# Routing a mixture of experts in four parts, with token lists kept in DRAM

## Chip, cores and metric

The kernel runs on one core of a Trainium2 chip. The metric is the device time of one launch in microseconds. The engines are TensorE (PE, with its weight loads shown as PEld), VectorE (DVE), ScalarE (ACT), GpSimd (POOL) and SyncE (SP, which issues most DMAs). Each engine runs its own instructions in program order and waits on semaphores.

## What is computed

The input is 8 batches of 512 tokens of 256 channels. Each batch goes through a linear attention layer, and then all 4096 tokens go through a feed-forward layer with one shared expert and 8 routed ones, of which every token uses two.

```python
x = x + layernorm(attention(layernorm(x)))          # per batch: q, k, v; state = k'v; ctx = q state; group norm; out
xf = layernorm(x).reshape(-1, 256)
shared = ffn(xf, shared_gate, shared_up, shared_down)   # ffn = (silu(x g') * (x u')) d', 704 hidden channels
probs = softmax(xf @ gate_w.T)                          # 8 experts
topw, topi = top_k(probs, 2);  topw = topw / topw.sum()
comb[token, topi] += topw
routed = sum over experts e of ffn(xf, e) * comb[:, e]
x = x + layernorm(shared + routed)
```

## The kernel before

The program has three stages. In the first, batch by batch, attention is computed, and beside it the shared expert of the batch before. The second, the **tail**, holds the shared expert of the last batch and all of the routing that is left. The third, the **routed stage**, works on 39 tiles (`NTILE`) of 256 token rows (`TW`), each of one expert. Tiles 0 to 7 belong to experts 1 to 8 in turn, so their weights are known without the routing; for the rest a table `eid` says which expert.

The order of the first two stages is written out by hand: `ORDER` for batches 1 to 6, `LAST_ORDER` for batch 7 and `TAIL`. Every engine walks the same list and does its share of each step. `("G", c)` is a gate and up projection on PE (12 matmuls, L911), `("H", c)` what ACT and DVE do with it (silu at L723, product at L1218, a high half at L737 and a low half at L1228), `("D", c)` the down projection on PE (L926). A batch has twelve of each. PE may start a G only when the product of the G two before is made, since there are two PSUM banks.

Four steps of a batch need a reciprocal root, which POOL computes (`root`, L605), in this order: LN1 at `ln1_stats`, the group norm GN at `ctx_norm`, LNO at `lno_stats` and LN2 at `x2`. DVE waits for them at L1207, L1414, L1428 and L1438. PE's output projection (L1015) needs what DVE makes at L1418. After LN2, ACT normalises the rows, which are then turned, give the routing logits and feed the next batch's shared expert.

The routing logits are in `logits`, a tile of 128 tokens to 8 columns. `route` runs on DVE in two parts: part 0 is batches 0 to 6 (28 tiles, 224 columns), part 1 is batch 7 (4 tiles, 32 columns). `route_probs` subtracts the maximum (L1317, L1318), ACT takes the exponential (L775), `route_top1` normalises and finds the first expert, `route_top2` the second and the weights. Part 0 runs in batch 7, part 1 at the end of it and in the tail. Then, in the tail:

- `route_slots`: PE counts with two matmuls (L1040, L1041), and DVE makes from them the place of each token in its expert's list (L1459 to L1474).
- `route_order` and `route_table`: the experts of tiles 8 to 38.
- `route_positions`: for each token its two places, split in a high and a low part.
- `one_hots` and `invert`, eight times: for four tiles of tokens DVE and POOL write one-hot matrices of the low part (L1527, L642), DVE those of the high part (L1530, 624 columns), and PE sums their products (L1052). The result has the token number of each place of all 39 tiles.
- `route_indices`: DVE turns that into indices for gathers (`idx`, L1550) and for scatters (`idx_s`, L1549).

POOL then gathers the rows of a tile by an indirect DMA (`gather_x`, L661), SP turns them by DMA, and the routed stage starts. The result of each tile is added to `acc_d` in DRAM by an indirect DMA with an add (`scatter`, L672). The profile names the DRAM tensor `xn2_d` as `xn_d` and `x2_d` as `x_d`.

During the first tiles of the routed stage the weights of experts 7 and 8 are still being laid out (`LATE`).

Of the kernel before, what the change touches and what calls it, by code (L numbers as in the profile page):

```python
# [8 lines left out]
F32 = mybir.dt.float32  # L9
# [7 lines left out]
P = 128  # L17
# [44 lines left out]
def turned_before(b, by_pe):  # L62
# [7 lines left out]
LAST_ORDER = [("ctx",), ("G", 0), ("ctx_out",), ("G", 1), ("channel_stats",), ("H", 0), ("group_mean",), ("H", 1), ("G", 2), ("group_var",),  # L70
# [5 lines left out]

TAIL = [("route_top1", 1), ("route_top2", 1), ("G", 0), ("H", 0), ("route_slots",), ("G", 1), ("G", 2), ("H", 1), ("D", 0), ("G", 3),
         ("D", 1), ("route_order",), ("G", 4), ("G", 5), ("H", 2), ("G", 6), ("G", 7), ("route_positions",), ("H", 3), ("route_table",),
         ("H", 4), ("G", 8), ("D", 2), ("one_hots", 0), ("G", 9), ("H", 5), ("H", 6), ("invert", 0), ("one_hots", 1), ("H", 7),
         ("invert", 1), ("D", 3), ("D", 4), ("one_hots", 2), ("invert", 2), ("one_hots", 3), ("H", 8), ("invert", 3), ("one_hots", 4),  # L80
         ("invert", 4), ("one_hots", 5), ("D", 5), ("invert", 5), ("G", 10), ("one_hots", 6), ("D", 6), ("H", 9), ("D", 7), ("invert", 6),
         ("one_hots", 7), ("invert", 7), ("G", 11), ("route_indices",), ("H", 10), ("D", 8), ("H", 11), ("D", 9), ("D", 10), ("D", 11)]
# [28 lines left out]
PROGRAM += [(b, step) for b in range(1, B - 1) for step in ORDER if b < NPRE or not step[0].startswith("prep")]  # L111
# [5 lines left out]
def build(nc, x_in, gu_in, dn_in, wqkv_in, wout_in, cols_in, out):  # L117
    xf = x_in.rearrange("b s d -> (b s) d")
    of = out.rearrange("b s d -> (b s) d")
    with ExitStack() as ctx:  # L120
# [10 lines left out]
        acc_d = nc.dram_tensor("acc_d", (TOK + TT * P, D), F32, kind="Internal").ap()  # L131

# [85 lines left out]
        OHB, POOL_H = 4, 1  # L218
        OHG = NTB // OHB
        OHR = 4  # L220
        oh_lo = [(wdn[:, (E - 1) * SLOT_DN + n * 1024:(E - 1) * SLOT_DN + (n + 1) * 1024] if n < OHR - 1 else attw[:, 2048:2560].bitcast(F16)).rearrange(
            "p (m h c) -> p m h c", m=2, h=OHB) for n in range(OHR)]
        OHI = 2 * OHB * NCOL
        OHS = 5
        oh_hi = [(spare[:, 2 * KD * S + n * OHI:2 * KD * S + (n + 1) * OHI] if n < OHS else xhl[:, (n - OHS) * OHI:(n - OHS + 1) * OHI]).rearrange(
            "p (m h c) -> p m h c", m=2, h=OHB) for n in range(OHG)]
# [90 lines left out]
        counted = sem("counted")  # L317
        eid_made = sem("eid_made")
# [81 lines left out]
        READ |= {KV_USES[t]: (kv_made, NT, t + 1) for t in range(NT)}  # L400

# [31 lines left out]
        def _(sp):  # L433
# [84 lines left out]
            sp.wait_ge(comb_made, 2)  # L518
            sp.dma_start(xn2_d[:, D:D + E].rearrange("(t p) e -> p t e", p=P), r_t.rearrange("p (t e) -> p t e", e=E)).then_inc(comb_stored, 16)
# [51 lines left out]
        def _(pool):  # L571
# [7 lines left out]
            g.iota(iota_i, pattern=[[1, P]], base=0, channel_multiplier=0).then_inc(link_p, 1)  # L579
            pool.wait_ge(link_p, 7)  # L580
# [1147 lines left out]
```

## Time and profile before

| | us |
|---|---|
| median of 3 runs | 857.74 (857.69 to 858.41) |
| the profiled execution | 856.2, of which span 854.4 |
| PE busy | 776.4 |
| DVE busy | 586.5 |
| ACT busy | 485.1 |
| POOL busy | 290.0 |

The profile is of one execution; times in it count from the start of its span. A batch of the first stage takes 40.95 us; batch 5 is at 223.4 to 264.3, batch 7 from 305.3 to 346.2, the tail to 396, and the routed stage's first matmul is at 402.6. An idle time in square brackets is that of the engine just before the row, with what ended it.

### The profile page before, as it was taken

What the parts mean: (1) busy time and instruction counts of PE and PEld (TensorE: products, weight loads), DVE (VectorE), ACT (ScalarE), POOL (GpSimd) and SP (SyncE); (2) the same over time, 40 slices, a digit from 0 to 9 for tenths busy, and PEclk for the clock granted to TensorE, in tenths of its full rate; (3) what the DMA queues carried; (4) which work ended last, traced back from release to release, by engine and by line L of the source; (5) the groups of instructions that cost most, each with busy time, mean ns of one, the idle gap of its engine ahead of it and who ended that gap; (6) DMA issues with size and microseconds to landing.
All of it is one profiled execution on the core that took longest, in us unless ns stands there. A gap on an engine that the chain in (4) does not pass through costs nothing.

```text
span 854.4 us, 20946 instructions
## 1 busy us (share of the span) xinstructions
PE 776.4 (91%) x6525; PEld 641.2 (75%) x6526; DVE 586.5 (69%) x1591; ACT 485.1 (57%) x1068; POOL 290.0 (34%) x316
## 2 busy tenths in 40 slices
PE   3679999999999998675899999999999999999991
PEld 1447777777777776554787888888888888888880
DVE  6668889898989888894787544555555555555553
ACT  2264848485857575522566555565656565656562
POOL 3011010101010100062265555555555555555542
PEclk9899999999999999987999999999999999999996
DMA  4104444454435342502244644646464646474843
GB/s 191 50 25 180 105 148 113 142 124 154 131 136 150 105 149 81 148 1 69 50 71 71 102 73 74 122 77 148 71 147 73 147 66 147 73 145 71 149 41 97
DMA packets 102690, 90.08 MB, mean 105 GB/s; under 512 B 63760, under 2 KB 94224, under 8 KB 101456
## 3 DMA queue, kind: packets, MB, share of 16 engines
q1 hardware_dynamic: 87648, 68.45, 28.0%
q0 software_dynamic: 14976, 20.78, 16.5%
q8 instruction: 38, 0.62, 0.3%
q14 instruction: 28, 0.23, 0.1%
HBM read 48.70 MB, written 27.39 MB: 89 GB/s over the span
## 4 chain that ended last, share of the span: by engine, by line
PE 73%; DVE 15%; ACT 5%; issue 3%; DMA 2%; POOL 1%; SPq 0%; ACTq 0%; DVEq 0%; POOLq 0%
PE ps L911 41%; PE ps L926 19%; PE ps L983 4%; PE ps L1015 3%; DVE wgu L1278 3%; PE ps L977 2%; ACT wgu L771 2%; DVE hf L1218 1%; DVE wdn L1278 1%; DVE st L1394 1%; PE ps L952 1%; DVE st L1198 1%; DVE wdn L1527 1%; PE ps L986 1%; DVE hT L1228 1%
## 5 line engine op out<-in xcount | busy, mean ns | idle before, releaser
L911 PE MATMUL ps<-xhl,wgu 128*128 128x256 f16 x3102 | 386.1, 274 | 12.2 <-DMA xhl<-attw 6.6
L911 PEld LDWEIGHTS ps<-xhl,wgu 128*128 (+1 forms) x3102 | 303.3, 98 | 55.7 <-issue 8.8
L1218 DVE SCALAR_TENSOR_TENSOR hf<-ps,sc,silu 128x256 f32<-128x256 f32 x330 | 159.6, 484 | 186.5 <-ACT silu L723 145.7
L926 PE MATMUL ps<-wdn,hT 128*128 (+1 forms) x1870 | 254.1, 274 | 11.3 <-DVE hT L1228 8.9
L723 ACT ACTIVATE silu<-ps,sc 128x256 f32<-128x256 f32 x275 | 130.4, 474 | 232.4 <-PE ps L911 215.5
L926 PEld LDWEIGHTS ps<-wdn,hT 128*128 128x128 f16 x1870 | 182.5, 98 | 37.3 <-DVE hT L1228 6.3
L672 POOL DMA_INDIRECT acc_d<-ysb,gst x78 | 128.7, 1650 | 44.5 <-POOL gst L668 30.9
L605 POOL TENSOR_TENSOR rstd<-ve,mhalf 128x4 f32<-128x4 f32 (+1 forms) x32 | 30.7, 960 | 297.5 <-DVE ve L1203 275.8
L1228 DVE TENSOR_TENSOR hT<-hf,hT 128x256 f16<-128x256 f32 x275 | 114.9, 418 | 1.7
L737 ACT CAST hT<-hf 128x256 f16<-128x256 f32 x275 | 109.7, 399 | 9.5 <-DVE hf L1218 7.8
L661 POOL DMA_INDIRECT attw<-xn_d,gst x78 | 80.1, 1027 | 44.5 <-POOL gst L657 32.6
L911 PE MATMUL ps<-wgu 128*128 128x256 f16 x528 | 68.4, 282 | 2.8 <-DVE hf L1218 2.8
L911 PEld LDWEIGHTS ps<-wgu 128*128 128x128 f16 x528 | 52.5, 101 | 15.9 <-DVE hf L1218 3.5
L983 PE MATMUL ps<-attw,att 128*128 128x512 f16 x192 | 46.7, 379 | 3.1 <-ACT att L815 3.1
L668 POOL COPY gst<-ones 128x2 int32 (+1 forms) x39 | 8.5, 217 | 102.2 <-ACT ysb L753 102.2
L726 ACT ACTIVATE silu<-ps,sc 64x256 f32<-64x256 f32 x55 | 25.7, 467 | 24.4 <-PE ps L911 23.0
L983 PEld LDWEIGHTS ps<-attw,att 128*128 128x128 f16 x192 | 18.7, 98 | 22.0 <-ACT att L815 3.6
L1015 PE MATMUL ps<-attw,att 128*128 128x256 f32 x128 | 33.7, 397 | 0.2 <-DVE att L1418 0.2
L753 ACT ACTIVATE ysb<-ps,yw 128x256 f32<-128x256 f32 x78 | 32.8, 474 | 1.5 <-PE ps L926 1.4
L1278 DVE SCALAR_TENSOR_TENSOR wgu<-wgu,pw 128x1408 f16<-128x1408 f32 x16 | 26.3, 1682 | 4.9 <-ACT wgu L771 4.9
L1230 DVE TENSOR_TENSOR hT<-hf,hT 64x256 f16<-64x256 f32 x55 | 23.2, 422 | 7.7 <-ACT hT L740 4.8
L1015 PEld LDWEIGHTS ps<-attw,att 128*128 128x128 f32 x128 | 22.7, 198 | 6.0 <-DVE att L1418 0.5
(239 smaller groups left out, 758.2 us busy)
## 6 DMA issues: line engine op xcount, KB each, us to landing
wgu<-in_gu SPq DMA_DIRECT2D x8, 1408.0 KB, 6.2
att<-in_x SPq DMA_DIRECT2D x16, 512.0 KB, 4.9
wdn<-in_dn SPq DMA_DIRECT2D x8, 768.0 KB, 8.1
x_d<-att SPq DMA_DIRECT2D x8, 512.0 KB, 2.9
xn_d<-wgu SPq DMA_DIRECT2D x8, 512.0 KB, 3.4
acc_d<-ysb SPq DMA_DIRECT2D x16, 256.0 KB, 3.3
att<-x_d SPq DMA_DIRECT2D x8, 512.0 KB
att<-acc_d SPq DMA_DIRECT2D x7, 512.0 KB
```

What stands on the lines that cost most here:

```text
L661: g.indirect_dma_start(xg[:, r, t, :], None, xn2_d[:, :], bass.IndirectOffsetOnAxis(ap=idxc[:, 2 * r + t:2 * r + t + 1], axis=0)).then_inc ...
L672: g.indirect_dma_start(acc_d, bass.IndirectOffsetOnAxis(ap=idxc[:, 4 + t:5 + t], axis=0), ysb[:, t * D:(t + 1) * D], None, compute_op=ALU. ...
L723: a.activation(silu[:, c % 2 * TW:(c % 2 + 1) * TW], gu_ps[c % 2][:, 0:TW], ACT.Silu, scale=scale_of(slot, 0)).then_inc(silu_made, 1)
L737: a.copy(o, h).then_inc(hi_made, 1)
L753: ins = a.activation(ysb[:, tt * D:(tt + 1) * D], y_bank(u, tt), ACT.Copy, scale=by)
L911: ins = te.matmul(o, slot_gu(slot, hw, k, j), x(hx, k), start=(n == 0), stop=(n == len(TERMS) - 1))
L926: ins = te.matmul(y_bank(u, tt), h(hh), slot_dn(slot, c, hw), start=(c == 0 and n == 0 and tt == 0), stop=(c == FC - 1 and n == 1 and tt = ...
L983: te.matmul(att_bank(KV_USES[t])[:, :], xq[:, hx, k, t * P:(t + 1) * P], wqkvT[:, hw, k, D:3 * D], start=(n == 0), stop=False)
L1015: te.matmul(att_bank(OUT + h)[:, (t % 2) * D:(t % 2 + 1) * D], qT[:, k, t * P:(t + 1) * P], woT[:, k, :], start=(k == 0), stop=False)
L1218: v.scalar_tensor_tensor(out=hf[lo:P, c % 2 * TW:(c % 2 + 1) * TW], in0=up, scalar=scale_of(slot, 1, lo, P), in1=silu[lo:P, c % 2 * TW:(c ...
L1228: v.tensor_tensor(lo, h, hi, ALU.subtract).then_inc(lo_made, 1)
L1278: v.scalar_tensor_tensor(out=piece_of(s, 1, n), in0=staged(gu, dn, n), scalar=pw[:, 4 + n // KD:5 + n // KD], in1=piece_of(s, 0, n), op0=A ...
```

## The change

The routing is cut into four parts: batches 0 to 2 (part 0, 12 tiles), 3 and 4 (part 1, 8 tiles), 5 and 6 (part 2, 8 tiles) and 7 (part 3, 4 tiles). Parts 0 and 1 are worked on in batches 3 to 6 (`EXTRA`), part 2 in batch 7, part 3 in the tail.

A token's place no longer depends on the counts of all batches: each expert has a fixed region of 4096 places in a new DRAM list `ids_d`. PE gives the rank in it (`ranks`: one matmul with `upper16`, one for each earlier batch with `bsum16`, some more for the tiles of the part), and `route_positions` works on a part as soon as it is ranked. For parts 0 to 2, POOL then writes the token numbers straight into the list, by two indirect DMAs with an add for each of the 28 tiles (`scatter_ids`). Each has 128 rows of 4 bytes. POOL's calls stand between its roots.

For part 3 one-hots remain, of four tiles only, and PE adds them to the list rows, which are read back by DMA. This happens in two pieces: columns 0 to 15, the first eight tiles of the routed stage, in the tail; columns 16 to 77 in the routed stage (`LATE`: tiles 2 and 3), after an indirect DMA has read the rows of the other tiles. In the tail the indices of the first eight tiles now come before `route_segments`, `route_order` and `route_table`. The combination weights are stored in four DMAs in place of one.

```diff
+PART_B = ((0, 3), (3, 5), (5, 7), (7, 8))
+EXTRA = {3: {("H", 1): [("route_probs", 0)], ("H", 3): [("route_norm", 0)], ("H", 6): [("route_top1", 0)]},
+         4: {("H", 1): [("route_top2", 0), ("route_slots", 0)], ("H", 3): [("route_positions", 0)], ("H", 6): [("route_weights", 0)],
+             ("ctx_norm",): scatters(0, 0, 1), ("lno_stats",): scatters(0, 1, 3), ("x2",): scatters(0, 3, 6)},
+         5: {("H", 1): [("route_probs", 1)], ("H", 3): [("route_norm", 1)], ("H", 6): [("route_top1", 1)],
+             ("ln1_stats",): scatters(0, 6, 7), ("ctx_norm",): scatters(0, 7, 8), ("lno_stats",): scatters(0, 8, 10), ("x2",): scatters(0, 10, 12)},
+         6: {("H", 1): [("route_top2", 1), ("route_slots", 1)], ("H", 3): [("route_positions", 1)], ("H", 6): [("route_weights", 1)],
+             ("ctx_norm",): scatters(1, 0, 1), ("lno_stats",): scatters(1, 1, 4), ("x2",): scatters(1, 4, 8)}}
...
+         ("route_positions", 2)] + scatters(2, 0, 3) + [("G", 8), ("D", 3), ("H", 6), ("x2",)] + scatters(2, 3, 8) + [
...
+LATE |= {(2, 2): ("one_hots", 0, 1), (2, 4): ("invert", 0, 1), (3, 0): ("indices", 0, 1)}
...
+            def scatter_ids(n, j):
+
+                pool.wait_ge(pos_made, n + 1)
+                if j == 0:
+                    pool.wait_ge(ids_cleared, 32)
+                wait(pool, ids_scattered[j % 2], 16 * 2 * (j // 2))
+                for m in range(2):
+                    g.indirect_dma_start(ids_d, bass.IndirectOffsetOnAxis(ap=posi[:, m * NTB + j:m * NTB + j + 1], axis=0), tokf[:, j:j + 1], None,
+                                         compute_op=ALU.add).then_inc(ids_scattered[j % 2], 16)
...
+            def ranks(n):
+
+                t0, t1 = PART[n]
+                pe.wait_ge(const_made, 9)
+                pe.wait_ge(m_made, n + 1)
...
```

**POOL, batch 6.** Before, its roots follow each other: LNO and LN2 of batch 5 with LN1 of batch 6, then GN of batch 6 (128x2), its LNO and LN2, and the same three of batch 7.

```order
L605 TENSOR_TENSOR rstd<-ve,mhalf 128x4 x3
L605 TENSOR_TENSOR rstd<-ve,mhalf 128x2
L605 TENSOR_TENSOR rstd<-ve,mhalf 128x4 x2
L605 TENSOR_TENSOR rstd<-ve,mhalf 128x2
L605 TENSOR_TENSOR rstd<-ve,mhalf 128x4 x2
```

Now, from LN1 of batch 6 through GN, LNO and LN2 to GN, LNO and LN2 of batch 7:

```order
L679 TENSOR_TENSOR rstd<-ve,mhalf 128x4
L679 TENSOR_TENSOR rstd<-ve,mhalf 128x2
L699 DMA ids_d<-tokf,posi 65536x1 x2
L679 TENSOR_TENSOR rstd<-ve,mhalf 128x4
L699 DMA ids_d<-tokf,posi 65536x1 x6
L679 TENSOR_TENSOR rstd<-ve,mhalf 128x4
L699 DMA ids_d<-tokf,posi 65536x1 x8
L679 TENSOR_TENSOR rstd<-ve,mhalf 128x2
L679 TENSOR_TENSOR rstd<-ve,mhalf 128x4
L699 DMA ids_d<-tokf,posi 65536x1 x6
L679 TENSOR_TENSOR rstd<-ve,mhalf 128x4
L699 DMA ids_d<-tokf,posi 65536x1 x10
```

Six indirect DMAs now stand between the roots LNO and LN2, in batch 6 and again in batch 7.

**PE, the same batch, from the third G to the fourth.** Before:

```order
L1004 MATMUL ps<-gst,mask 128x4
L911 MATMUL ps<-wgu 128x256 x12
L926 MATMUL ps<-wdn,hT 128x256 x6
L911 MATMUL ps<-wgu 128x256 x12
L1008 MATMUL ps<-gst,mask 128x2
```

Now:

```order
L1141 MATMUL ps<-gst,mask 128x4
L1008 MATMUL ps<-wgu 128x256 x12
L1057 MATMUL ps<-wgu 128x64
L1059 MATMUL ps<-wgu,ones 128x64 x3
L1061 MATMUL ps<-wgu,ones 128x56
L1061 MATMUL ps<-wgu,ones 128x48
L1061 MATMUL ps<-wgu,ones 128x40
L1061 MATMUL ps<-wgu,ones 128x32
L1061 MATMUL ps<-wgu,ones 128x24
L1061 MATMUL ps<-wgu,ones 128x16
L1061 MATMUL ps<-wgu,ones 128x8
L1023 MATMUL ps<-wdn,hT 128x256 x6
```

The rank matmuls stand ahead of a down projection, and wait for DVE's second choice of the part.

**DVE, from the end of batch 7 into the tail.** Before, 25 rows of routing (here the first six) lie ahead of the first product of the tail's shared expert:

```order
L1230 TENSOR_TENSOR hT<-hf,hT 64x256
L1317 TENSOR_REDUCE small<-logits 128x4
L1318 TENSOR_TENSOR attw<-logits,small 128x32
L1321 TENSOR_REDUCE small<-attw 128x4
L1322 RECIPROCAL small<-small 128x4
L1323 TENSOR_TENSOR attw<-attw,small 128x32
L1309 TENSOR_REDUCE small<-attw 128x4
```

Now five rows do, and the first choice comes behind the product:

```order
L1451 TENSOR_REDUCE small<-logits 128x4
L1452 TENSOR_TENSOR wdn<-logits,small 128x32
L1455 TENSOR_REDUCE small<-wdn 128x4
L1456 RECIPROCAL small<-small 128x4
L1457 TENSOR_TENSOR wdn<-wdn,small 128x32
L1353 SCALAR_TENSOR_TENSOR hf<-ps,sc,silu 128x256
L1443 TENSOR_REDUCE small<-wdn 128x4
```

## Rows read from the trace of the kernel before

**Rows 1.** The page, part 1: busy time, share of the span, instructions

```profile
PE 776.4 (91%) x6525; PEld 641.2 (75%) x6526; DVE 586.5 (69%) x1591; ACT 485.1 (57%) x1068; POOL 290.0 (34%) x316
```

**Rows 2.** Windows: length, busy PE, PEld, DVE, ACT, POOL, granted clock, DMA, GB/s

```profile
223.40:264.30 40.90, 40.60 (x319) 31.03 (x318) 36.38 (x97) 27.29 (x55) 3.71 (x4) 1.00 0.43 133
305.30:346.20 40.90, 35.80 (x312) 29.06 (x310) 35.13 (x96) 27.34 (x53) 2.71 (x3) 0.96 0.34 114
346.20:402.60 56.40, 34.55 (x280) 25.94 (x281) 44.15 (x167) 16.91 (x38) 19.85 (x22) 0.85 0.28 76
```

**Rows 3.** Timeline of DVE, batch 5: start, us, instruction, idle before

```profile
239.93 1.00 DVE L1418 TENSOR_SCALAR att<-att,gst 128x512 f32<-128x512 f32 x2
...
250.72 1.23 DVE L1433 TENSOR_TENSOR att<-att 128x1024 f32<-128x1024 f32 x1 [2.00 <-ACT att L815]
...
255.57 0.15 DVE L1438 SCALAR_TENSOR_TENSOR attw<-mv,rstd 128x4 f32<-128x4 f32 x1
```

**Rows 4.** Timeline of PE, batch 5: the output projection

```profile
240.98 1.13 PE L1015 MATMUL ps<-attw,att 128*128 128x256 f32 x4
```

**Rows 5.** Timeline of POOL, batch 5: LN1 with GN, LNO, LN2

```profile
236.44 1.70 POOL L605 TENSOR_TENSOR rstd<-ve,mhalf 128x4 f32<-128x4 f32 x2 [22.30 <-DVE ve L1203]
247.51 1.01 POOL L605 TENSOR_TENSOR rstd<-ve,mhalf 128x4 f32<-128x4 f32 x1 [9.38 <-DVE ve L1203]
254.08 1.01 POOL L605 TENSOR_TENSOR rstd<-ve,mhalf 128x4 f32<-128x4 f32 x1 [5.56 <-DVE ve L1203]
```

**Rows 6.** Timeline of DVE: routing steps of 224 and of 32 columns

```profile
328.96 0.39 DVE L1310 TENSOR_TENSOR attw<-attw,small 128x224 f32<-128x224 f32 x1
...
350.12 0.19 DVE L1310 TENSOR_TENSOR attw<-attw,small 128x32 f32<-128x32 f32 x1
350.34 0.19 DVE L1311 TENSOR_TENSOR attw<-attw,rev 128x32 f32<-128x32 f32 x1
```

**Rows 7.** Timeline of ACT: the exponential and its table load

```profile
347.68 1.28 ACT L775 ACT_TABLE_LOAD   x1
348.97 0.23 ACT L775 ACTIVATE attw<-attw 128x32 f32<-128x32 f32 x1
```

**Rows 8.** Indirect DMAs on POOL, lines 661 and 672: duration ns min/median/max

```profile
L661 POOL DMA_INDIRECT attw<-xn_d,gst x78: 949/987/1673, 393.9 to 806.3; - x78
L672 POOL DMA_INDIRECT acc_d<-ysb,gst x78: 1539/1616/2597, 427.6 to 840.4; - x78
```

**Rows 9.** Timelines of POOL and SP: the last scatter, the load behind it

```profile
840.37 1.54 POOL L672 DMA_INDIRECT acc_d<-ysb,gst  x1 [0.30 <-issue]
843.95 0.80 SPq L562 DMA_DIRECT2D att<-acc_d  x2
```

**Rows 10.** Timeline of DVE, batch 7: an H step, then the wait for LN2

```profile
335.74 0.48 DVE L1218 SCALAR_TENSOR_TENSOR hf<-ps,sc,silu 128x256 f32<-128x256 f32 x1
336.14 0.41 DVE L1228 TENSOR_TENSOR hT<-hf,hT 128x256 f16<-128x256 f32 x1
336.47 0.15 DVE L1438 SCALAR_TENSOR_TENSOR attw<-mv,rstd 128x4 f32<-128x4 f32 x1
```

**Rows 11.** Timeline of DVE: last routing logits, first product, last index of the tail

```profile
348.15 0.19 DVE L1317 TENSOR_REDUCE small<-logits 128x4 f32<-128x32 f32 x1
...
353.90 0.48 DVE L1218 SCALAR_TENSOR_TENSOR hf<-ps,sc,silu 128x256 f32<-128x256 f32 x1
...
392.48 0.24 DVE L1550 SCALAR_TENSOR_TENSOR idx<-attw 128x78 int32<-128x78 f32 x1
```

**Rows 12.** Timeline of PE: start of the routed stage

```profile
402.62 5.56 PE L911 MATMUL ps<-xhl,wgu 128*128 128x256 f16 x36 [6.60 <-DMA xhl<-attw]
```

**Rows 13.** Windows of batch 7, columns as in rows 2

```profile
335.00:337.00 2.00, 0.46 (x5) 0.42 (x6) 1.86 (x7) 1.42 (x4) 1.00 (x1) 1.00 0.17 58
337.00:338.50 1.50, 1.50 (x11) 1.11 (x9) 1.40 (x4) 1.50 (x4) 0.00 (x0) 0.63 0.52 175
338.50:340.00 1.50, 1.50 (x9) 1.03 (x8) 1.36 (x6) 0.41 (x2) 0.00 (x0) 0.50 0.00 0
```

More of the change, by code:

```diff
@@ new lines, with scatters @@
+PART = tuple((NT * lo, NT * hi) for lo, hi in PART_B)
+def scatters(n, lo, hi):
+    return [("scatter_ids", n, j) for j in range(PART[n][0] + lo, PART[n][0] + hi)]
+EXTRA = {3: {("H", 1): [("route_probs", 0)], ("H", 3): [("route_norm", 0)], ("H", 6): [("route_top1", 0)]},
[5 more added lines that the diff above has]
+             ("ctx_norm",): scatters(1, 0, 1), ("lno_stats",): scatters(1, 1, 4), ("x2",): scatters(1, 4, 8)}}
@@ new lines, in order_of @@
+def order_of(b):
+    steps = []
+    for step in ORDER:
+        if b < NPRE or not step[0].startswith("prep"):
+            steps += [step] + EXTRA.get(b, {}).get(step, [])
+    return steps
+LAST_ORDER = [("ctx",), ("G", 0), ("ctx_out",), ("G", 1), ("channel_stats",), ("H", 0), ("group_mean",), ("H", 1), ("route_probs", 2), ("G", 2),
+         ("group_var",), ("G", 3), ("H", 2), ("route_norm", 2), ("G", 4), ("ctx_norm",), ("H", 3), ("H", 4), ("out",), ("route_top1", 2), ("G", 5),
+         ("lno_stats",), ("D", 0), ("G", 6), ("route_top2", 2), ("route_slots", 2), ("H", 5), ("G", 7), ("D", 1), ("D", 2), ("lno_apply",),
+         ("route_positions", 2)] + scatters(2, 0, 3) + [("G", 8), ("D", 3), ("H", 6), ("x2",)] + scatters(2, 3, 8) + [
+         ("H", 7), ("D", 4), ("H", 8), ("D", 5), ("ln2_apply",), ("route_weights", 2), ("H", 9), ("D", 6), ("G", 9), ("D", 7),
+         ("turn2",), ("G", 10), ("xhl",), ("H", 10), ("rows2",), ("G", 11), ("D", 8), ("logits",), ("D", 9), ("logits_out",), ("D", 10),
+         ("H", 11), ("route_probs", 3), ("D", 11)]
@@ L110 @@
 PROGRAM = [(step[0], step[1:]) for step in START]
-PROGRAM += [(b, step) for b in range(1, B - 1) for step in ORDER if b < NPRE or not step[0].startswith("prep")]
+PROGRAM += [(b, step) for b in range(1, B - 1) for step in order_of(b)]
 PROGRAM += [(B - 1, step) for step in LAST_ORDER]
@@ L219, in build @@
[L219 to L226, printed above, removed]
+        OHB, POOL_H = NT, 1
@@ L1036, in _ @@
                 if kind == "route_slots":
-                    pe.wait_ge(m_made, 2)
-                    x2_ready(pe, B - 1)
-                    te.matmul(att_ps[0][:, 0:256], upper[:, :], r_m, start=True, stop=True)
-                    te.matmul(att_ps[0][:, 256:512], ones[:, :], r_m, start=True, stop=True).then_inc(counted, 1)
+                    ranks(step[1])
+                if kind == "route_counts":
+                    pe.wait_ge(logits_made, B)
+                    for b in range(B):
+                        ins = te.matmul(att_ps[3][:, E * b:B * E].rearrange("p (t e) -> p t e", e=E), ones16[:, :], each(bsum16[:, E * b:E * b + E], B - b),
+                                        start=(b == 0), stop=(b == B - 1))
+                    ins.then_inc(counted, 1)
                 if kind == "route_order":
@@ L1045, in _ @@
                 if kind == "invert":
-                    for h in range(OHB):
-                        j = OHB * step[1] + h
-                        pe.wait_ge(onehot_made, step[1] + 1)
-                        pe.wait_ge(onehot_lo_made, POOL_H * step[1] + max(1, h - (OHB - POOL_H) + 1))
-                        for m in range(2):
-                            ins = te.matmul(att_ps[1][:, 0:NCOL], oh_lo[step[1] % OHR][:, m, h, :], oh_hi[step[1]][:, m, h, :],
-                                            start=(j == 0 and m == 0), stop=(j == NTB - 1 and m == 1))
-                    ins.then_inc(onehot_used, 1)
-            pe.wait_ge(eid_made, 1)
+                    invert(step[1])
             def routed(i, r, slot, before, later=None):
```

291 lines of the change are left out of this document (196 added, 95 removed), and 8 rows, old and new, of tables (LAST_ORDER, TAIL).

## The prediction

> **What bounds the kernel now.** I read the page first: PE is busy for 776.4 us of the span of 854.4, far ahead of DVE's 586.5 [rows 1]. So time can be won only where PE idles. The windows by stage say where [rows 2]: in a full batch PE is busy for 40.60 of 40.90 us, in batch 7 for 35.80 of 40.90, and between the end of batch 7 and the routed stage for 34.55 of 56.40 us, 22 us idle, at a granted clock of 0.85. That gap is what the change is about. The same windows show its danger: in the full batches nothing is idle that could take more work in the wrong place. The timelines of DVE and PE there are read for the slack between them. DVE ends the normalised context at 240.93 [rows 3], PE's output projection starts at 240.98 [rows 4]: no slack. DVE's only long wait is 2.00 us for ACT, at 250.72 [rows 3]. POOL's roots are read last: LN1 and GN are one merged row, LNO starts at 247.51, and LN2 at 254.08, so 5.56 us lie free between these two [rows 5].
>
> **Routing steps put into batches 3 to 6.** A linked DVE step of 32 columns is followed by the next after 0.22 us; one of 224 columns takes 0.39 and with the link 0.42 [rows 6]. Between them, 64 columns cost 0.25 and 96 columns 0.29. In each batch what stands after H 1 and H 3 lies ahead of the context norm, where there is no slack, so it stalls PE for its length. What stands after H 6 lies ahead of LNO's use, where 0.2 us is free; the 2.00 us wait for ACT comes behind and moves along. PE, at 40.60 of 40.90, gives nothing back.
> - Batch 3, 96 columns: maximum, subtraction, exponential, three steps of norm: 0.8 on the path beside the exponential; the first choice, five steps, 1.4 less 0.2. The exponential brings a table load of 1.28 [rows 7] and a second for the return to silu; most of it runs beside DVE's statistics, and I take 0.6. Sum 2.6.
> - Batch 4: eight steps of second choice, 2.3, for which PE's rank matmuls wait; positions 1.75; weights 1.65 less 0.2. Sum 5.5. The rank matmuls themselves, some 0.5, fit behind DVE's next stop.
> - Batch 5, 64 columns: 0.6, 0.7 and 1.1, sum 2.4. Batch 6: 2.0, 1.25 and 1.35, sum 4.6.
>
> Together 15.1 us. Were all absorbed by DVE's idle time of 4.5 us a batch (40.90 less 36.38 [rows 2]), 1.1 would be left; these are the ends. I take the upper one, because the row at 250.72 shows where that idle time is: behind the insertions.
>
> For the tables, the Trainium skill (ScalarE: Activation LUTs, What ACT_TABLE_LOAD costs) gives 1283 ns and then a drain of about 1380 ns for each switch. The trace has the first and not the second: the exponential starts at 348.97, where the load ends [rows 7]. By the page the four extra switches would add 5.5 us more; by the row they add nothing beyond the above.
>
> **POOL's scatters.** The trace has no scatter of 4-byte rows. Its nearest rows are the gather of 128 rows, 987 ns, and the scatter of 128 rows with an add, 1616 ns [rows 8], each 0.30 behind the one before [rows 9]. I take the second, since it has the same form with an add; so 1.92 us each, 3.84 a tile; the lower bound is 1.28.
> - Batch 4, two tiles between LNO and LN2: from 248.5 (batch 5's times), 7.7 us, root to 257.3; DVE wants it at 255.57 [rows 3] plus 1.35 of new steps. Stall 0.4.
> - Batch 5, one tile between LN1 and GN: LN1's root ends at 237.9, two scatters 3.8, root 0.7: 242.5 against 240.6. Stall 1.8, and 0.7 at LN2.
> - Batch 6, three tiles between LNO and LN2: 11.5 us, root to 261.1 against 256.7. Stall 4.3. DVE stands at L1438, and behind it are the staging maxima and H 9, so PE stands too.
>
> Sum 7.2 (at the lower bound 0.8). A PE stall as long as batch 6's also costs clock: after 2 us in which PE was busy for 0.46, it got 0.63 and 0.50 of 2.4 GHz, so 1.2 GHz for most of three us [rows 13]. I add 1.7.
>
> **Batch 7 and tail.** Positions of part 2 end at 331.4; six scatters to 342.9, root to 344.0. In the trace DVE passes L1438 at 336.47 [rows 10]; with 1.0 of longer steps before, it would be 337.5, so DVE stands 6.5 us. From there to the last logits' maximum at 348.15 [rows 11] were 11.7 us. 3.8 of routing leave that stretch, which gives 7.9 if DVE paces it and 11.7 if not; following ACT's rows, the turn, the high and low halves, logits and the last H by their places I get 10.1. So this point T0 moves from 348.15 to 354.1.
>
> Behind T0 the old tail ran to 402.62 [rows 12], 54.5 us. The new one, on DVE:
> - to the first product 3.8: exponential, table back to silu, silu. It was 5.75 (353.90 [rows 11]), with 25 routing steps in front, of which five stay.
> - H 0 to H 3 with an H step at 0.85 (0.48 and 0.41, overlapping [rows 10]), first choice 1.1, second 1.8, weights 1.45, positions 2.0, one-hots of four tiles 2.0: 11.3, so 15.1 after T0, 369.2.
> - the list must be there: five tiles of scatters behind 344.1 end at 363.3, landing 2.0 (841.91 to 843.95 [rows 9]), loading about 2.4: 367.7. It is, by 1.5.
> - product on PE 0.9, indices 1.8: at 371.9. In the old tail the last index was made at 392.72 and PE began 9.9 later [rows 11, 12]; the same here is 381.8, hidden behind what is left.
> - eight H steps 7.2, segments, order and table 5.2, the last round trips and down projections 2.2.
>
> Sum 32.4, so PE goes on at 386.6: 16.0 earlier. It also starts warm: the old start took 5.56 us for 36 matmuls [rows 12], some 1.6 more than at full clock. The second piece of the indices adds about 2.7 us of DVE and 0.7 of PE in tiles 2 and 3 of the routed stage, mostly beside PE: 1.0 (bounds 0 and 3.4). Four stores of weights, the clearing of the list and the constants lie beside other work: 0.
>
> **Sum:** 15.1 + 7.2 + 1.7 - 16.0 - 1.6 + 1.0 = +7.4 us. On the profiled execution that is a span of 861.8; on the median, which is 1.5 above that execution, 857.7 + 7.4 = 865.1.
>
> **Rivals.**
> - **Cheap scatters (faster).** If a 4-byte scatter costs the gather's 1.28, the stalls of batches 4 to 6 are 0.8, the clock term goes, LN2's root in batch 7 is at 340.2, T0 at 350.3, the routed stage at 382.8: 15.1 + 0.8 - 19.8 - 1.6 + 1.0 = -4.5, so 853.2. The two sums cross at 1.53 us a scatter. For it: rows of 4 bytes and not 1 KB. Against: the gather's rows are as long as the scatter's and it is still the cheaper, so length is not what tells them apart.
> - **DVE's idle time absorbs the steps.** Then 15.1 becomes 1.1 and the sum -6.6: 851.1. For it: 4.5 us idle a batch. Against: rows 3 and 4, no slack at the context norm.
> - **Contention at SBUF.** The longest scatter took 2597 ns [rows 8]. If all did beside a DVE that is busy for 36 of 41 us, 2.9 each: the stalls are 22.6 in place of 7.2, LN2 of batch 7 comes 5.9 later, the list is late for the product by 8.2: 895. Against: the median is 1616 while DVE works too. The Trainium skill (GPSIMD Engine Reference, Key points) says that POOL shares its SBUF interfaces with VectorE, with contention in some modes and with two SBUF inputs. The trace's medians do not bear it out for this instruction.
> - **Even.** A scatter cost near 1.5, or half of the steps absorbed with dear scatters: 857.7.
>
> **Chances.** Forecast 0.52, cheap scatters 0.20, absorption 0.13, contention 0.07, even 0.08. Faster by over 0.2% (1.7 us, about what a measurement can tell) is the second and third with a little of the first, 0.35; within it 0.09; slower 0.56. The range takes in the two faster cases with their own errors and ends at 874, where the forecast has 5 us more for further clock losses; it leaves out contention. The forecast's own range is 859 to 873.
>
> **What would show it.** Right: batches 3 to 6 longer than 40.95 by some 2.6, 6, 5 and 9 us; scatters near 1.6 us; DVE idle at its LN2 wait in batches 6 and 7; first routed matmul about 34 us after the last logits' maximum. Wrong: scatters at 1.0 or less, batches that keep 41 us, or a tail bound by something else, such as the list's load.

## The result and the profile after

The changed kernel takes **946.5 us** (median of 6 runs, 941.5 to 958.3) against 857.7 us before: a ratio of 1.102, 95% interval 1.099 to 1.106. Ratio and interval go by the fast runs of both kernels alone, so they differ a little from the quotient of the medians. The forecast was 865.1 us, 849 to 874. The sign was right, the size was not: 89 us lost where 7 were forecast.

The profiled execution of the changed kernel took 954.2 us, its span is 952.4. That execution is 8 us above the median, so the stages below differ by 98 us in all and not by 89. I cut both traces at the first matmul of the routing logits of each batch, and at the first matmul of the routed stage:

| stage, us | before | after | forecast of the change |
|---|---|---|---|
| batch 3 | 40.95 | 43.54 | +2.6 |
| batch 4 | 40.95 | 65.14 | +5.9 |
| batch 5 | 40.96 | 73.07 | +4.9 |
| batch 6 | 41.09 | 58.78 | +8.9 |
| batch 7 | 35.06 | 45.44 | +6 |
| tail, to the routed stage | 58.29 | 66.86 | -22 |
| routed stage | 451.78 | 454.26 | -0.6 |

The clock term of 1.7 stands in no row. Batch 3, which has routing steps and no scatter, is as forecast. The loss begins with the first scatters in batch 4. Four windows of the changed kernel (length, busy PE, PEld, DVE, ACT, POOL, granted clock, DMA share, GB/s), batches 3, 4, 5 and the tail, answer to [rows 2]:

```profile
145.31:188.85 43.54, 41.05 (x318) 30.90 (x317) 38.76 (x107) 30.03 (x58) 3.72 (x4) 1.00 0.39 116
188.85:253.99 65.14, 43.82 (x331) 32.79 (x329) 45.79 (x124) 29.68 (x59) 23.99 (x16) 0.88 0.88 91
253.99:327.06 73.07, 47.19 (x317) 34.42 (x318) 39.13 (x106) 30.05 (x57) 22.82 (x16) 0.80 1.05 80
431.28:498.14 66.86, 32.48 (x276) 25.08 (x274) 26.37 (x109) 17.35 (x39) 19.25 (x17) 0.74 0.52 69
```

PE's busy time grew by only 3 and 7 us in batches 4 and 5, and it stands for a third of batch 5. What is new is the last but one column: the DMA engines are busy all the time (0.88, 1.05; 0.43 in [rows 2]) and move less (91 and 80 GB/s, 133 there). The share adds up the times of packets, and since it passes 1, some of them overlap: the time of a packet is not time in which an engine does nothing else. The queues between 200 and 300 us name whose packets fill that time, first of the kernel before, then after (packets, MB, share of 16 engines; transfers with KB each and median us to landing):

```profile
q1 hardware_dynamic: 11090, 11.58, 37.5%
wgu<-in_gu SPq DMA_DIRECT2D x2, 1408.0 KB, 6.2
wdn<-in_dn SPq DMA_DIRECT2D x2, 768.0 KB, 7.9
```

```profile
q0 software_dynamic: 2610, 0.01, 51.0%
q1 hardware_dynamic: 8320, 7.19, 42.1%
wgu<-in_gu SPq DMA_DIRECT2D x1, 1408.0 KB, 12.4
wdn<-in_dn SPq DMA_DIRECT2D x1, 768.0 KB, 19.3
```

The scatters' queue moved 10 KB, and its packets' times come to half of all 16 engines. That is 51% of 1600 us over 2610 packets: 0.31 us a packet, the mean of the queue (0.24 between 190 and 440 us). The weights beside it took 12.4 and 19.3 us in place of 6.2 and 7.9. On POOL the same shows as waits. First the group of the page, then POOL in batch 4 (start, length, instruction, idle before and who ended it):

```profile
L699 POOL DMA_INDIRECT ids_d<-tokf,posi x56 | 90.8, 1622 | 85.7 <-DMA ids_d<-tokf,posi 68.0
```

```profile
221.03 1.54 POOL L699 DMA_INDIRECT ids_d<-tokf,posi  x1 [0.30 <-issue]
222.03 1.61 POOL L679 TENSOR_TENSOR rstd<-ve,mhalf 128x4 f32<-128x4 f32 x1
231.32 1.60 POOL L699 DMA_INDIRECT ids_d<-tokf,posi  x1 [7.67 <-DMA ids_d<-tokf,posi]
...
237.65 1.54 POOL L699 DMA_INDIRECT ids_d<-tokf,posi  x1 [2.89 <-DMA ids_d<-tokf,posi]
...
246.99 2.08 POOL L699 DMA_INDIRECT ids_d<-tokf,posi  x1 [5.94 <-DMA ids_d<-tokf,posi]
```

The cost of issue is about what I took, a mean of 1622 ns (median 1542) for a median of 1616 [rows 8]. But a pair waits for the pair two tiles back, and that has not landed: 68.0 us in 16 waits of the whole execution. Who pays further on (engine and line, releaser, us in all, times, longest), between 188 and 440 us:

```profile
DVE attw L1626 <- POOL rstd L679: 29.3, 4, 12.4
PE ps L1044 <- DVE diag L1391: 28.8, 3, 12.4
PE ps L1168 <- DMA wgu<-wgu: 9.8, 1, 9.8
PE ps L1168 <- DMA xhl<-wgu: 8.3, 1, 8.3
```

In the tail the list's load on SP starts only at 470.14, 12.9 us after the last scatter left POOL (455.7 + 1.5), and PE waits 24.0 us for it:

```profile
470.14 0.35 SPq L585 DMA_DIRECT2D wgu<-ids_d  x1
```

```profile
471.68 0.99 PE L1078 MATMUL ps<-ident,wgu 8*128 8x8 f32 x4 [24.02 <-DMA wgu<-ids_d]
```

### The profile page after: what moved, and what is told of

It is laid out like the page before. It is cut to its first block, busy times and chain, and to the rows that moved or that the text cites. A ratio compares the mean times of both kernels' runs of the same rounds, so it can differ in the third digit from the quotient of the medians.

```text
span 952.4 us, 21043 instructions
## 1 busy us (share of the span) xinstructions
PE 790.4 (83%) x6528; PEld 647.8 (68%) x6537; DVE 582.0 (61%) x1611; ACT 489.3 (51%) x1074; POOL 370.8 (39%) x363
## 4 chain that ended last, share of the span: by engine, by line
PE 53%; DMA 17%; DVE 11%; issue 8%; ACT 5%; POOL 5%; SPq 0%; ACTq 0%; another core or an unknown queue 0%; POOLq 0%; DVEq 0%
PE ps L1008 32%; PE ps L1023 15%; DMA ids_d<-tokf,posi 14%; POOL ids_d L699 3%; PE ps L1120 2%; DMA wgu<-wgu 2%; DVE hf L1353 2%; DVE wgu L1413 1%; PE ps L1152 1%; ACT wgu L863 1%; POOL rstd L679 1%; PE ps L1114 1%; DVE st L1333 1%; DVE wdn L1413 1%; DVE hT L1363 1%
## 5 line engine op out<-in xcount | busy, mean ns | idle before, releaser
L1023 PE MATMUL ps<-wdn,hT 128*128 (+1 forms) x1870 | 257.7, 276 | 9.5 <-DVE hT L1363 5.9
L679 POOL TENSOR_TENSOR rstd<-ve,mhalf 128x4 f32<-128x4 f32 (+1 forms) x32 | 34.5, 1079 | 241.0 <-DVE ve L1338 238.4
L699 POOL DMA_INDIRECT ids_d<-tokf,posi x56 | 90.8, 1622 | 85.7 <-DMA ids_d<-tokf,posi 68.0
L1008 PE MATMUL ps<-wgu 128*128 128x256 f16 x528 | 69.5, 285 | 3.7 <-DVE hf L1353 3.6
L752 POOL COPY gst<-attw 128x2 int32 (+1 forms) x39 | 8.4, 215 | 100.6 <-ACT ysb L843 100.6
L923 ACT ACTIVATE att<-att,attw,rstd 128x256 f32<-128x256 f32 x32 | 16.6, 588 | 39.5 <-DVE attw L1626 31.1
L1044 PE MATMUL ps<-diag,ones 128*128 128x256 bf16 x10 | 3.2, 322 | 39.8 <-DVE diag L1391 30.2
L741 POOL COPY gst<-idx 128x2 int32 (+1 forms) x39 | 16.7, 429 | 46.2 <-DVE attw L1531 15.7
```

The source lines that it names most:

```text
L679: g.tensor_tensor(rstd[n][:, 0:cols], ve[n][:, 0:cols], mhalf[:, 0:cols], ALU.pow).then_inc(rstd_made[n], 1)
L699: g.indirect_dma_start(ids_d, bass.IndirectOffsetOnAxis(ap=posi[:, m * NTB + j:m * NTB + j + 1], axis=0), tokf[:, j:j + 1], None, compute_ ...
L1008: ins = te.matmul(o, slot_gu(slot, hw, k, j), x(hx, k), start=(n == 0), stop=(n == len(TERMS) - 1))
L1023: ins = te.matmul(y_bank(u, tt), h(hh), slot_dn(slot, c, hw), start=(c == 0 and n == 0 and tt == 0), stop=(c == FC - 1 and n == 1 and tt = ...
```

## The experiments

Theory A: the scatters, by their slow landing, are the loss; A1 blames the add, A2 the small packet, A3 neighbouring words. Theory B: the inserted steps and the new tail cost much more than I summed.

### Without scatters

Both scatters of a tile and the three waits on them are left out:

```
             def scatter_ids(n, j):
                 ...
-                for m in range(2):
-                    g.indirect_dma_start(ids_d, ...)
```

> Leaves out the 56 scatters of token numbers into the list in DRAM and the waits on them; everything else of the changed kernel stays. The list then holds zeros for batches 0 to 6, so the routed stage gathers row 0 for them and its outputs mean nothing; the time up to the routed stage is what counts. Theory A (the scatters, by their slow landing, are the whole cause of the loss): what is left is the sum's other terms, 15.1 of routing steps, about -19.8 in batch 7 and the tail (LN2's root no longer late), -1.6 warm start, +1.0 = about -5 us, so about 852.5 us on the median, batches 3 to 6 at 43.5, 46.5, 43.4 and 45.6 us, DMA share of these batches near 0.45. Rival B (the inserted DVE steps or the new tail cost much more than I summed): well above 870 us, with batch 4 still above 50 us.

Measured: 862.4 us (861.4 to 867.9), ratio 1.006, interval 1.004 to 1.009. Stages from batch 3: 43.56, 48.50, 43.30, 46.72, 36.17, 44.33, 452.96. So 84 of the 89 us hang on the scatters, and A holds in the main. It is also 10 us above my 852.5, and B has that much: batch 4 with 2.1 more than the sum's terms, batch 6 with 1.0, the tail with 8. In batch 4, PE stood 2.22 us ahead of the rank matmuls. The row names no releaser, but DVE's last step of the second choice (L1460), which writes their operand, ends at 199.62:

```profile
199.72 0.20 PE L1050 MATMUL ps<-wgu 128*128 128x96 bf16 x1 [2.22 <-issue]
```

The tail, in rows of DVE (last logits' maximum, first hidden step, last index of the first piece, the count's result, two late hidden steps), then two late gate and up projections of PE and the start of the routed stage:

```profile
368.63 0.19 DVE L1444 TENSOR_REDUCE small<-logits 128x4 f32<-128x32 f32 x1
...
372.55 0.48 DVE L1346 SCALAR_TENSOR_TENSOR hf<-ps,sc,silu 128x256 f32<-128x256 f32 x1 [2.21 <-ACT silu L806]
...
385.55 0.18 DVE L1524 TENSOR_TENSOR attw<-attw 128x16 int32<-128x16 f32 x1
...
391.83 0.23 DVE L1653 TENSOR_SCALAR lohi_i<-ps 128x64 int32<-128x64 f32 x1 [4.31 <-PE ps L1173]
...
400.98 0.48 DVE L1346 SCALAR_TENSOR_TENSOR hf<-ps,sc,silu 128x256 f32<-128x256 f32 x1 [2.46 <-ACT silu L806]
...
403.57 0.49 DVE L1346 SCALAR_TENSOR_TENSOR hf<-ps,sc,silu 128x256 f32<-128x256 f32 x1 [1.77 <-ACT silu L806]
```

```profile
387.76 2.77 PE L1001 MATMUL ps<-wgu 128*128 128x256 f16 x12
...
397.83 2.51 PE L1001 MATMUL ps<-wgu 128*128 128x256 f16 x12
...
409.14 3.03 PE L1001 MATMUL ps<-xhl,wgu 128*128 128x256 f16 x26
```

From the maximum's start (368.63), the forecast's T0, the first hidden step is 3.9 away (forecast 3.8) and the indices are ready after 17.1 (forecast 15.1 + 0.9 + 1.8 = 17.8). From there to PE's start are 23.4 us, where I had 14.6; the whole is 40.5 in place of 32.4. DVE waits in that stretch: 4.31, 2.46, 1.77. PE waited too, and two of its projections that come soon after such waits took 2.77 and 2.51 us where later ones take 1.47; the granted clock was 0.77 from 385.7 to 397.8 and 0.85 from there on, against 0.96 ahead of the indices. The forecast of this stretch had no term for the clock.

### Written, not added

```
-    g.indirect_dma_start(ids_d, ..., tokf[:, j:j + 1], None, compute_op=ALU.add)
+    g.indirect_dma_start(ids_d, ..., tokf[:, j:j + 1], None)
```

> One change: the scatters write the token number instead of adding it (positions never repeat, the list is cleared, so the list is the same). Theory A1 (the read, add and write of each 4-byte word in DRAM makes the landing long): landing falls to the 2 to 3 us that I had taken, the DMA share of batches 4 to 6 falls from about 0.9 to about 0.5, POOL's waits for the landing (68.0 us in all) nearly go, and the time is about 860 us. Rival A2 (a packet of 4 bytes is slow however it is written): landing stays at 10 us or more, DMA share near 0.9, time within 10 us of 946.

Measured: 931.8 us (930.0 to 932.6), ratio 1.086, interval 1.083 to 1.088: 15 us faster, 4 us outside A2's 10. So the add, with its longer instruction on POOL, is some 15 of the 89 us; A1 falls as the main cause. POOL's instruction fell from 1542 to 962 ns (medians) and the packets from 144 to 32 a scatter, yet POOL still waited 69.5 us for landings. Between 200 and 300 us the scatters' own packets now come to little, and the other queue's to much:

```profile
q1 hardware_dynamic: 10870, 8.87, 57.5%
q0 software_dynamic: 768, 0.01, 1.8%
```

### Entries 512, 64, 16 and 8 bytes apart, and rows of 512 bytes

The indices are multiplied by 128, 16, 4 or 2, and the scatters, still with the add, go to a tensor of their own:

```
-    v.tensor_copy(both(posi[:, :]), both(posf))
+    v.tensor_scalar(both(posi[:, :]), both(posf), 128.0, None, ALU.mult)
...
-    g.indirect_dma_start(ids_d, ...
+    g.indirect_dma_start(far_d, ...
```

> The same scatters with the add, but into another tensor in which every entry stands 512 bytes from the next (the indices are multiplied by 128), so no two entries share a line of memory. The list that is read stays zero, so outputs mean nothing; the cost of the scatters is what counts. Theory A3 (adds to neighbouring words wait for each other): landing falls under 4 us, time about 860 us. Rivals A1 and A2 (add itself, or the small packet itself): landing unchanged, time 940 to 955 us.

> The same 56 scatters with the add at the same row numbers, but each row is 512 bytes of a constant instead of 4 bytes, into another tensor; the list that is read stays zero, so outputs mean nothing. If the add to neighbouring 4-byte words is what is slow (A3), 512-byte rows land faster than the 4-byte ones although they move 128 times as much: under 5 us, time about 865 us. If each packet with an add costs a fixed time (A1), landing is as in the changed kernel or longer, time 945 to 980 us.

> As the run with entries 512 bytes apart, but 64 bytes apart (indices times 16, with the add, into another tensor; the list that is read stays zero, so outputs mean nothing). Theory A3a (words collide when they share 64 bytes or less): as at 512 bytes, 873 to 878 us, POOL's waits for the landing near zero. Rival A3b (they collide within a larger block, 128 to 512 bytes): between, 885 to 930 us.

> The same with entries 16 bytes apart (indices times 4), so a block of 64 bytes holds 4 entries and not 16; outputs mean nothing. A3a: collisions are fewer than in the changed kernel but not gone, 880 to 925 us. If words collide only with direct neighbours within 16 bytes: as at 64 bytes, 875 us.

> Entries 8 bytes apart (indices times 2, with the add, into another tensor; the list that is read stays zero, so outputs mean nothing). At 16 bytes nothing was left of the collisions (878.6 us). If only words that touch collide: about 878 us again. If two entries within a block of 16 bytes collide: 885 to 920 us.

Measured, one run each: 512 bytes apart 875.6 us; rows of 512 bytes, next to each other, 877.5; 64 bytes apart 880.8; 16 bytes 878.6; 8 bytes 900.1. The scatters' queue between 200 and 300 us with entries 512, 16 and 8 bytes apart:

```profile
q0 software_dynamic: 3600, 0.01, 12.7%
```

```profile
q0 software_dynamic: 3600, 0.01, 15.5%
```

```profile
q0 software_dynamic: 3456, 0.01, 35.0%
```

As time of one packet, share times 1600 us over packets: 0.056, 0.069 and 0.162 us, and 0.31 in the changed kernel, where they stand 4 bytes apart. From issue to landing, with 512 bytes and with 8:

```profile
DMA to landing us min/median/max: 2.9/3.3/8.1
```

```profile
DMA to landing us min/median/max: 4.1/7.5/10.5
```

So it is neither the small packet (A2) nor the add alone (A1). Entries 4 and 8 bytes apart cost, the closer the more (A3); from 16 bytes on the runs lie within 5 us, in no order of distance, which one run each can't tell apart. Whether what matters is the distance or a shared aligned block of 16 bytes was not tried. My guess of a block of 64 bytes (A3a) is not borne out: it wanted the run with 16 bytes (878.6) well above the one with 64 (880.8). The row of 512 bytes says it from the other side: 128 times the data with the same indices, 2 us above entries 512 bytes apart. All of these kernels lie above the 860 and 865 us that I expected of A3: 13 us are left against the kernel without scatters, which are POOL's issue and the late roots (below).

### The layout changed inside the list

Within each tile's 256 entries entry r goes to 17 r mod 256; the routed stage doesn't care in which order a tile's tokens stand.

```
+    v.tensor_scalar(both(lohi_i), both(posf), 17.0, None, ALU.mult)
+    v.tensor_scalar(both(posi), both(posi), ~(TW - 1), None, ALU.bitwise_and)
+    v.tensor_scalar(both(lohi_i), both(lohi_i), TW - 1, None, ALU.bitwise_and)
+    v.tensor_tensor(both(posi), both(posi), both(lohi_i), ALU.bitwise_or)
```

> The list stays where it is, but within each tile's 256 entries (1 KB) entry r stands at 17 r mod 256, so that the ranks that one scatter writes next to each other lie 68 bytes apart; the order of tokens within a tile changes nothing in the outputs. Costs three more small steps of DVE in each positions step, about 0.6 us each, 2.4 us in all. A3a: some 16 entries of a list fall on 16 different 64-byte lines: close to the run with 512 bytes, 875 to 880 us. A3b (a larger block): 900 to 950 us.

Measured: 885.9 us, one run, where 875 to 880 was expected. In the list's own tensor, with the add and with POOL's issue unchanged, the layout alone takes 60 us off, so it was not the other tensor that made the runs above fast. The rest against 512 bytes may be ranks 15 apart, which this factor puts side by side again (17 x 15 = 255), beside the new steps.

> Entries at 17 r mod 256 and written instead of added. The scatter that only writes took 1064 ns on POOL where the one with the add took 1622: 56 times 0.56 us less. If the spread takes the collisions away (A3a), the stalls behind POOL are about those of my rival with cheap scatters: about 866 us. If not (A3b), 900 to 930 us.

Measured: 880.1 us (877.3 to 883.0), ratio 1.023; 866 was expected. In the profiled execution, the longest of the four, ACT waited 5.92 us in batch 6 and 6.95 at the start of the tail, during rows of eight and ten scatters, for something the trace calls remote; its tail is 7.9 us longer than that of the kernel with the add (52.61 and 44.71). No such wait of over 1.5 us shows in the other runs, the last one below, with fourteen scatters within 18 us, among them. What it is stays open.

### Steps where DVE waits anyway

Scatters left out; the routing steps of batches 3 to 6 stand ahead of the addition for x2:

```
-  4: {("H", 1): [("route_top2", 0), ("route_slots", 0)], ("H", 3): [("route_positions", 0)], ("H", 6): [("route_weights", 0)]}
+  4: {("G", 8): [("route_top2", 0)], ("kv", 0): [("route_slots", 0)], ("H", 9): [("route_positions", 0)]}
```

> On the run without scatters (862.4 us): the inserted routing steps stand elsewhere, most of them ahead of the addition for x2, where DVE waits 2.00 us for ACT in each batch (norm and first choice in batch 3, second choice in 4 and 6, norm, first choice and weights in 5), the positions behind H 9. My forecast's reading: the idle time lies behind the insertions, so steps put right ahead of the wait are absorbed, up to 2.0 us in each of batches 3 to 6: 855 us. Rival: the wait is not idle time that can be used, since what comes behind ACT is late then anyway or PE stands for the rank matmuls: 860 to 865 us. Outputs mean nothing, as without scatters.

Measured: 855.2 us (853.7 to 856.7), where 855 was expected. Batches 3 to 6 took 41.63, 43.08, 43.03 and 41.91: 5.7 us over the kernel before in place of 18.1. Not all of the 12.4 stays won: batch 7 took 39.39 (36.17 without the move) and the tail 45.35 (44.33), so 8.2 are left. What holds batch 7 up is not shown. DVE before (L1433) and in this kernel (L1611), the addition for x2 in batch 4:

```profile
209.76 1.23 DVE L1433 TENSOR_TENSOR att<-att 128x1024 f32<-128x1024 f32 x1 [2.00 <-ACT att L815]
```

```profile
209.37 0.16 DVE L1606 SCALAR_TENSOR_TENSOR nmr<-mv,rstd 128x4 f32<-128x4 f32 x1 [0.20 <-POOL rstd L675]
209.45 0.25 DVE L1451 SCALAR_TENSOR_TENSOR wdn<-wdn 128x96 f32<-128x96 f32 x1
...
211.48 0.32 DVE L1457 TENSOR_REDUCE wgu<-wgu 128x24 bf16<-128x96 bf16 x1
211.72 1.21 DVE L1611 TENSOR_TENSOR att<-att 128x1024 f32<-128x1024 f32 x1
```

Eight steps stand in the hole, and the addition starts with no wait.

### The tail in another order

Scatters left out; seven hidden steps ahead of the first product in place of four, six of them ahead of the positions.

```
- ... ("G", 4), ("H", 3), ("D", 2), ("route_positions", 3), ("one_hots", 0), ("G", 5), ("invert", 0) ...
+ ... ("G", 6), ("H", 5), ("D", 4), ("route_positions", 3), ("one_hots", 0), ("G", 7), ("H", 6), ("D", 5), ("invert", 0) ...
```

> On the run without scatters (862.4 us): only the order of the tail changes, with six H steps ahead of the first product in place of four and the counting, order and table between later ones. The tail from the last logits' maximum to the routed stage took 40.3 us there, where I had summed 32.4. Theory T1 (what stands behind the indices is paced by PE at 12 + 6 matmuls a step, 2.3 us, not by DVE at 0.85 as I took it, while PE stands idle ahead of them): indices come about 2 us later, the routed stage starts 3 to 6 us earlier: 857 to 859 us. Rival T2 (the gathers and transposes behind the indices set the start): no earlier, 862 to 865 us. Outputs mean nothing, as without scatters.

Measured: 860.3 us (857.0 to 864.2) against 862.4, the intervals of the ratios overlap, so the time alone decides nothing. In the trace the routed stage starts 37.8 us behind T0, not 40.5 (the 40.3 of the expectation count from the maximum's end). The indices came 23.7 behind it, not 17.1, and PE began 14.1 us after them. So T1 holds in its direction: hidden steps moved ahead shorten the end, by 2.7 us where it wanted 3 to 6, and the indices paid for it with 6.6 us, not 2. T2 does not: PE's last down projections run up to 406.36 and the routed stage follows at 406.20 with no wait for a gather or a transpose.

### Eight tiles of scatters in flight

The changed kernel with eight semaphores in place of two:

```
-    wait(pool, ids_scattered[j % 2], 16 * 2 * (j // 2))
+    wait(pool, ids_scattered[j % 8], 16 * 2 * (j // 8))
```

> The changed kernel with eight semaphores in place of two, so that a tile's pair of scatters waits for the pair eight tiles back and not two; adds and layout as in the changed kernel. Theory W (POOL's 68.0 us of waits for the landing, and the roots behind them, are the loss): those waits nearly go, batches 4 and 5 fall from 65 and 73 us to some 48, the tail still waits for the last landing: 900 to 915 us. Rival M (the collisions hold up the DMA engines themselves, and every other transfer with them, whoever waits): no wait of POOL, but the same total of landings; weights, x and the list come late all the same: 935 to 960 us.

Measured: 944.3 us (938.9 to 947.5), ratio 1.101, interval 1.096 to 1.106: as the changed kernel. Its landings, and who waited between 190 and 440 us:

```profile
DMA to landing us min/median/max: 4.2/14.9/27.7
```

```profile
ACT att L923 <- DMA x_d<-att: 47.2, 4, 19.3
...
PE ps L1044 <- DVE diag L1391: 39.0, 3, 18.8
...
PE ps L1168 <- DMA xhl<-wgu: 11.5, 1, 11.5
...
DVE attw L1626 <- POOL rstd L679: 9.6, 3, 5.0
```

POOL waits for no landing any more, and its roots are late by 9.6 us and not 29.3. In their place ACT waits 47.2 us until x2 is stored. Theory W falls, M holds in its main point: the transfers that run beside the scatters are late, whoever waits. It does not hold for all transfers. Between 200 and 300 us the stores of x2 took 20.5 us to land (2.9 in the kernel before), the load of the weights as long as before:

```profile
x_d<-att SPq DMA_DIRECT2D x2, 512.0 KB, 20.5
wgu<-in_gu SPq DMA_DIRECT2D x1, 1408.0 KB, 6.0
```

That load was issued at 256.30, when the scatters of batch 4 had landed: between 256 and 266 us the trace has no packet of theirs. Between 206 and 245 us, where the store falls, their packets come to 79% of the 16 engines. In the changed kernel, whose scatters are spread out by POOL's waits, the load of batch 5 had scatters beside it (285 of their packets between 248 and 265 us, 10% of the engines' time, and 88% for the other queue) and took 12.4 us. Whether the engines themselves are held or the memory behind them no run tells apart.

### A version with all of it

Entries at 223 r mod 256 (ranks up to 30 apart stand at least 32 bytes apart), written and not added, the steps in DVE's wait, six hidden steps ahead of the product in place of four, scatters behind the roots:

```
+  4: {..., ("logits",): scatters(0, 0, 4)},
+  5: {..., ("ctx_norm",): scatters(0, 4, 8), ("lno_stats",): scatters(0, 8, 10), ("x2",): scatters(0, 10, 12)},
+  6: {..., ("logits",): scatters(1, 0, 4)}}
```

> A whole version made from what the runs showed: entries at 223 r mod 256 within each tile of the list (ranks up to 30 apart stand at least 32 bytes apart), written and not added; the routing steps of batches 3 to 6 ahead of the wait for ACT, as in the run that had them there; one H step more ahead of the first product; scatters behind the roots, at most ten in a row, none between LN1 and the context norm's root. Sum: 855.2 (steps moved, no scatters) + 2.5 (three more small steps in each positions step) + 2 (roots that wait for a scatter) - 1 (tail) = 859 us, within 2 us of the kernel before. Rival: bursts of scatters delay instruction loading, as ACT's waits of 5.9 and 6.9 us in the run with entries mixed and written suggested; then 865 to 872 us.

Measured: **853.8 us** (852.4 to 854.9) against 857.1 for the kernel before beside it: a ratio of 0.9955, interval 0.9941 to 0.9969. It beats both kernels, the one before by 0.45%; 859 was expected. The expectation's "at most ten in a row" does not hold for this kernel: sixteen scatters follow LN2's root of batch 7, fourteen of them within 18 us, and the loss of its rival did not come. Batch 4 and the tail:

```profile
190.25:233.79 43.54, 41.19 (x332) 31.39 (x329) 40.28 (x117) 27.31 (x55) 8.87 (x10) 1.00 0.46 140
...
360.74:399.11 38.37, 28.02 (x276) 22.07 (x274) 26.98 (x113) 17.35 (x39) 16.47 (x19) 1.00 0.44 120
```

The routing steps and scatters add 7.5 us to batches 3 to 6 and 5.6 to batch 7, and the tail is 19.9 shorter than before. What lies ahead of batch 3 took 3.3 us longer in this execution and the routed stage 1.2, which makes -2.3 in all. How much of the step from 880 us comes from the factor, the places of the scatters and the places of the steps was not taken apart.

## Why the prediction was wrong, point by point

- **What bounds the kernel.** Right: PE's idle time in the tail was there to win; the last version won about half of it (22 us idle before, 10 then). The resource that then ran out, the DMA engines, stood in [rows 2] with a share of 0.43, but no term asked what the scatters would take of it.
- **Routing steps, 15.1.** Without scatters the four batches grew by 2.6, 7.6, 2.3 and 5.6, in all 18.1; forecast 2.6, 5.5, 2.4, 4.6. The choice of the upper end was right, and so was its reason: with steps put into the wait at 250.72 in [rows 3] these batches cost 5.7 in place of 18.1 (net of batch 7 and the tail, 8.2 less). Mis-sized by 2 was batch 4, where PE stood 2.22 for the ranks' operand.
- **POOL's scatters, 7.2, and clock, 1.7.** Issue took 1542 ns (median; 1622 mean) where the row had 1616 (1650 mean). With entries 512 bytes apart, where landings hardly wait, DVE stood 0.9, 4.4 and 5.0 us for LN2's root in batches 5, 6 and 7; forecast 0.7, 4.3 and 6.5. That kernel is 13 us above the one without scatters; by my terms 7.2 + 1.7 + 3.8 (batch 7 and tail) = 12.7. This step was right in sum; in parts, batch 4 was 1.3 shorter than without scatters (forecast 0.4 longer) and batch 7 with the tail 5.7 longer (forecast 3.8).
- **The landing, 2.0.** This is the step that failed, and with it the DMA engines' time, which had no term. I took 841.91 to 843.95 of [rows 9], a scatter of rows of 1 KB, for the landing of 4-byte words, gave it no bounds, and so took the wait for the pair two tiles back as free. The landing is 3.3 us with entries 512 bytes apart and 14.9 with eight tiles in flight in the real layout (medians); in the changed kernel POOL waited 68.0 us for it. And transfers of weights, x and x2 that run beside it are late: 12.4 us for a weight load in place of 6.2. Changed kernel less entries 512 bytes apart: 946.5 - 875.6 = 71 us, in no term and in none of my rivals. That the time hangs on the distance of neighbouring entries, none of the rows of the kernel before could show.
- **The tail, 32.4 behind the last maximum.** Up to the indices it took 17.1 for 17.8. (The terms listed from H 0 to H 3 add up to 11.75 and not to 11.3, so 17.8 should have been 18.25.) Behind them I had 14.6 and it took 23.4: I priced a hidden step at DVE's 0.85, but PE gives each its 12 and 6 matmuls, 1.47 and 0.82 us, and with ACT in between DVE waits. Some 2.3 us more are the two projections at 2.77 and 2.51, at a granted clock of 0.77 to 0.85. So 8 us of the gain never came, even without a scatter.
- **Warm start, -1.6, and second piece, +1.0.** The first 36 matmuls took 4.12 us in place of 5.56 [rows 12], -1.4. The routed stage of the kernel without scatters is 1.2 longer than before, so the second piece costs about 2.6, within its bounds of 0 and 3.4.
- **Rivals.** Contention at SBUF was the only one with a large loss (895, less than half of what came), by the wrong mechanism: POOL's instruction kept its median. Absorption was true for steps placed in the wait, not for these. The cheap scatter was not this kernel's; in the last version one costs 958 ns.
- **The pages.** The exponential starts 0.02 us after its table load here too, and the load 0.02 us after the instruction before it (367.74 + 0.40):

```profile
368.16 1.28 ACT L860 ACT_TABLE_LOAD   x1
369.46 0.23 ACT L860 ACTIVATE wdn<-wdn 128x32 f32<-128x32 f32 x1
```

So the drain of about 1380 ns that the Trainium skill (ScalarE: Activation LUTs, What ACT_TABLE_LOAD costs) gives doesn't show in the kernel without scatters. The Trainium skill (DMA: Bandwidth & Descriptors, Specifications) says that below 512 bytes a transfer does a read-modify-write. That alone does not tell these kernels apart: all but the one with rows of 512 bytes wrote 4 bytes a row, and they took from 875.6 to 946.5 us by the distance of the rows.

## What to carry to other kernels

Before many small scatters go to DRAM, ask how far apart neighbouring entries land, and price the landing and the DMA engines' time as terms of their own: here the packets of a queue that moved 10 KB came to half of it. Where the order within a block is free and its size a power of two, multiply the place by an odd factor modulo the block, and look which ranks the factor puts side by side again. Put steps of no hurry right ahead of an engine's existing wait, and price a stretch by the engine that paces it, not by the one whose rows are at hand.

## What the runs showed of the hardware

- The mean time of a packet of an adding scatter of 4-byte rows, between 200 and 300 us: 0.31 us with entries 4 bytes apart, 0.162 with 8, 0.069 with 16, 0.056 with 512. Nothing was tried between 8 and 16 bytes.
- Without the add a scatter of 128 rows is 32 packets and not 144, and 962 ns on POOL and not 1542 (medians). With neighbours side by side its own queue shows 1.8% of the engines' time, and the other queue 57.5% for 8.87 MB between 200 and 300 us, where the kernel before needed 37.5% for 11.58: by this reading the hold-up then shows in the others' packets.
- The limit is not the number of scatters in flight: with eight tiles in place of two the time was the same, 944.3 and 946.5 us. A weight load of 1.4 MB with none of them beside it still took 6.0 us there.
